# A graph network with gated updates: another order of the products with S, of the normalising and of the last step's VectorE work

## The chip, the cores and the metric

The kernel runs on one core of a Trainium2 chip. The metric is the device time of one execution in microseconds (us). Engines are named as in the profile: PE is TensorE, ACT is ScalarE, DVE is VectorE, POOL is GpSimd, SP is the queue that issues most DMAs.

## The reference

Eight graphs of 1024 nodes with 128 channels pass four layers of message passing with a gated unit (GRU); then the input is added and each node is normalised over its channels.

```python
h = x
for i in range(L):                                   # L = 4
    hw = jnp.einsum('bnc,cd->bnd', h, weight[i])
    m = jnp.einsum('bjn,bjd->bnd', adj, hw)          # 1024 x 1024 adjacency, 0 or 1
    gx, gh = m @ w_ih[i].T + b_ih[i], h @ w_hh[i].T + b_hh[i]
    r = sigmoid(xr + hr); z = sigmoid(xz + hz); n = tanh(xn + r * hn)
    h = (1 - z) * n + z * h
y = x + h * mask[:, :, None]
out = (y - mean(y)) / sqrt(var(y) + 1e-5)            # over the 128 channels
```

## The kernel before

**Tiling and stages.** Graphs go in four pairs (`p` = 0 to 3, here also "pair 1" to "pair 4"). A pair takes eight steps `g` = 0 to 7: layer `g // 2` of graph `g % 2`, so that one graph's matmuls run while the other's state is made and turned. The layer's weight is folded into the input weights (`wx`) at the start. Every value that TensorE reads is split in two, a rounded high part and the remainder (`nat_hi`, `nat_lo` for the state in natural layout; `hT_hi`, `hT_lo` for the transposed state; `S_hi`, `S_lo` for the aggregated state), because one pass of TensorE rounds its operands.

**A step on TensorE.** `aggregate` makes S, the neighbours' sum, for both halves of 512 nodes: 32 matmuls with 128x512 results (line 465). Then `gates` runs for each half `h`: nine matmuls with the state, into p_r, p_z and p_hn, and nine with S, into p_r, p_xn and p_z (`product`, lines 476 to 478, three each). The four result banks are shared by both halves, so the second half's first matmul into a bank waits until the first half's reader has emptied it: `r_act`, `z_act`, `t_mul`, `t_add`.

**What the other engines do with a half.** ScalarE: sigmoid of p_r, sigmoid of p_z, and, after VectorE, tanh (`gate`, line 657). VectorE: (p_hn + bias) * r (line 1094), that plus p_xn (line 1100). POOL: h - n (line 1212), times z (line 1216). VectorE: `new_state`, n + that (line 923), `turn`, a transposition of 32x32 blocks (line 865); SP sends it to DRAM (`bounce`) and back (`low`, also called `back`) in natural layout, ScalarE and VectorE split it (`take_back`). ScalarE and VectorE also make S_hi (line 602) and S_lo (`s_low`, line 808), hT_hi and hT_lo, and ScalarE copies or checks the adjacency of the next graphs (`take_adj`, `check_adj`).

**The end of a graph.** In steps 7 (graph 0) and 0 of the next pair (graph 1) VectorE adds the input (`residual`, line 881), takes statistics (line 892) and moments (line 901), POOL raises the variance to the power -1/2 (line 1195). `normalise` (line 912) runs at the end of VectorE's steps 1 (graph 0 of the former pair) and 2 (graph 1), eight instructions each; SP stores in steps 2 and 3 and loads the next x into `y` in step 4.

**The last step** of the last pair has its own order by hand (`last_step` on PE, ACT and DVE): there S is made for half 0, its gates, then for half 1. Graph 0's normalising is ScalarE's work: `shift` (line 1013) is made by VectorE from POOL's power, and ScalarE waits for it (`shift_made`) with two blocks ahead of the sigmoids of half 1 (lines 671 and 693).

**What sets the order.** All engines work through their instructions in the order of the program and wait on semaphores; nothing reorders them. SP's queue is one such order too.

Of the kernel before, what the change touches and what calls it, by code (L numbers as in the profile page):

```python
# [34 lines left out]
def gnn_kernel(nc, x, adj, nodemask, weight, w_ih, w_hh, b_ih, b_hh, out):  # L35
    B, N, C = x.shape
    L = weight.shape[0]
    NB = N // P
# [10 lines left out]
    with ctx:  # L49
# [219 lines left out]
        def _(sp):  # L269
# [30 lines left out]

            def send_back(p, g, first):

                for h in range(2):
                    n = STEPS * p + g
                    sp.wait_ge(h_turned, HS * p + 2 * g + h + 1)
                    if not (first and g == 0):
                        sp.wait_ge(bounce_back[h], 16 * n)
                    sp.dma_start(bounce[h], turned[:, h]).then_inc(bounce_out[h], 16)

                    if first and g == 0:  # L310
                        sp.wait_ge(low_first, 1)
                    elif g == 0:
                        sp.wait_ge(y_added, 4 * (p - 1) + 2 + h + 1)
                    elif g == STEPS - 1:
                        sp.wait_ge(y_added, 4 * p + h + 1)
                    else:
                        sp.wait_ge(nat_split, HS_IN * p + 2 * (g - 1) + h + 1)
                    sp.wait_ge(bounce_out[h], 16 * (STEPS * p + g + 1))
                    sp.dma_start(back[:, h].rearrange("p q j c -> p q (j c)"),
                                 bounce[h].rearrange("(q r) (m f) -> (r m) q f", q=Q, m=Q)).then_inc(bounce_back[h], 16)  # L320

            def body(p, first, last):
                for g in range(STEPS):
# [4 lines left out]
                    if g in (2, 3):  # L328
                        if not last:
                            next_adj(p, 0, first, range((g - 2) * HB, (g - 1) * HB))  # L330
                        if not first:
                            store(p - 1, g - 2)
                    elif g == 4:
# [3 lines left out]
                        for s in range(2):  # L337
                            if not first:

                                sp.wait_ge(out_stored[s], 16 * p)  # L340
                            sp.dma_start(y[:, s], x_v[2 * p + s]).then_inc(y_loaded[s], 16)
                    elif last:
# [33 lines left out]
        def _(pe):  # L376
# [103 lines left out]
            def gates(p, g, h, first, between=None):  # L480
# [22 lines left out]
                product(p_r, (wx_hi, wx_lo), l, 0, fed, False, True).then_inc(r_done, 1)  # L503
                if prior:
                    pe.wait_ge(t_add, HS * p + k)
                product(p_xn, (wx_hi, wx_lo), l, 2, fed, True, True).then_inc(xn_done, 1)
                product(p_z, (wx_hi, wx_lo), l, 1, fed, False, True).then_inc(z_done, 1)
# [297 lines left out]
        def _(dve):  # L805
# [103 lines left out]
            def normalise(p, s):  # L909
                dve.wait_ge(rstd_made, 2 * p + s + 1)  # L910
                for j in range(NB):
                    last = nc.vector.tensor_scalar(y[:, s, j], y[:, s, j], mv[:, s, j, 0:1], rstd[:, s, j:j + 1],  # L912
                                                   ALU.subtract, ALU.mult)
                last.then_inc(y_normed, 1)
# [80 lines left out]
            def last_step(p):  # L995
                g = STEPS - 1
                k = 2 * g
                whole = slice(0, H)
                new_state(p, g - 1, 1)
                turn(p, g - 1, 1)  # L1000
                s_low(p, g, 0)
# [3 lines left out]
                residual(p, 0, 1)  # L1005
                for h in range(2):
                    wait_stats(p, 0, h)
                    moments(0, h)
                variance_eps(p, 0)
                s_low(p, g, 1)  # L1010
                new_state(p, g, 0)
                dve.wait_ge(rstd_made, B - 1)
# [34 lines left out]
            def body(p, first, last):  # L1047
# [4 lines left out]
                def fill():  # L1052
                    if checks:
                        check_adj(*checks.pop(0))
                        if not checks:
                            mask_first()

                for g in range(STEPS):
# [25 lines left out]
                    for h in range(2):  # L1084
# [16 lines left out]
                        if h == 0:  # L1101
# [4 lines left out]
                            elif g:  # L1106
                                take_back(p, g - 1, 1)
                            if last and g == STEPS - 2:
# [16 lines left out]
                    if 1 <= g <= 2 and not first:  # L1125

                        normalise(p - 1, g - 1)
# [135 lines left out]
```

## Time and profile before

| | |
|---|---|
| time, median of 3 runs | 562.23 us (562.16 to 562.79) |
| the profiled execution | 565.01 us, its span 563.1 us |
| PE busy | 528.3 us, 94% |
| DVE busy | 416.0 us, 74% |
| ACT busy | 357.1 us, 63% |
| POOL busy | 213.3 us, 38% |
| mean granted clock of PE | 0.987 of full speed |

The span is the time from the first to the last instruction that the profiler recorded; the profiled execution's own time has the start and the end around it. A matmul's busy time is longer than its share of the stream, since matmuls overlap: 390 ns each, while the next one starts 0.23 us after it. So the busy share of PE hides short stalls, and distances between starts show them.

### The profile page before, as it was taken

The page shows a single profiled execution, that of the slowest core. Times are in us where ns is not written, and L with a number is a line of the kernel's source. Part 1 is how long each engine was busy: PE and PEld are TensorE (multiplying, and loading weights), DVE is VectorE, ACT ScalarE, POOL GpSimd, SP SyncE. Part 2 cuts the span into 40 slices and gives each one's busy share as a digit, 9 for nine tenths or more (in the row PEclk, how much of TensorE's full clock was granted, in tenths as well). Part 3 has the DMA queues.
Part 4 walks back from the last instruction along what each step waited for, and adds up shares of the span by engine and source line. Part 5 has one row for each costly group of instructions (what it writes and reads, how often), then busy time and mean ns, then how long its engine had stood idle before and what let it go on. Part 6 is the DMA issues. An engine that isn't in the chain of part 4 may idle for free.

```text
span 563.1 us, 7447 instructions
## 1 busy us (share of the span) xinstructions
PE 528.3 (94%) x2288; PEld 419.1 (74%) x2288; DVE 416.0 (74%) x737; ACT 357.1 (63%) x568; POOL 213.3 (38%) x161
## 2 busy tenths in 40 slices
PE   5898999999999999999999999999999999999981
PEld 4566788778887777778787777777888777887660
DVE  3997766765888786676788777667688778767586
ACT  3856767647776667755877576755886764544332
POOL 0143333333365333322366431332365522433332
PEclk9999999999999999999999999999999999999986
DMA  7952445443722177544541176643471133341112
GB/s 228 393 185 75 154 182 177 142 131 131 275 81 76 56 244 243 150 130 150 192 182 56 56 240 196 197 148 113 134 258 38 57 112 112 101 120 61 59 36 78
DMA packets 79808, 80.93 MB, mean 144 GB/s; under 512 B 3656, under 2 KB 63648, under 8 KB 79776
## 3 DMA queue, kind: packets, MB, share of 16 engines
q1 hardware_dynamic: 79504, 80.41, 43.1%
q8 instruction: 16, 0.26, 0.2%
q10 hardware_dynamic: 272, 0.13, 0.1%
q14 instruction: 16, 0.13, 0.1%
HBM read 60.08 MB, written 20.45 MB: 143 GB/s over the span
## 4 chain that ended last, share of the span: by engine, by line
PE 45%; DVE 24%; ACT 13%; issue 7%; DMA 5%; POOL 3%; SPq 2%; DVEq 1%; ACTq 0%; POOLq 0%
PE p_S L465 18%; ACT work L657 6%; ACT adj_hi L602 4%; PE p_z L476 4%; DVE y L912 3%; DVE work L1094 3%; PE p_r L476 3%; PE p_z L478 3%; PE p_z L477 3%; DVE work L1100 3%; PE p_r L478 3%; DMA low<-bounce 3%; PE p_r L477 3%; DVE hT L923 2%; DVE hT_lo L808 2%
## 5 line engine op out<-in xcount | busy, mean ns | idle before, releaser
L1212 POOL TENSOR_TENSOR work<-hT,work 128x512 f32<-128x512 f32 x63 | 82.7, 1313 | 295.3 <-ACT work L657 295.3
L465 PE MATMUL p_S<-adj_hi,nat_hi 128*128 128x512 f32 x480 | 187.3, 390 | 0.0
L465 PE MATMUL p_S<-adj_hi,nat_lo 128*128 128x512 f32 x480 | 186.8, 389 | 0.0
L465 PEld LDWEIGHTS p_S<-adj_hi,nat_lo 128*128 128x128 f32 x480 | 90.1, 188 | 18.6
L465 PEld LDWEIGHTS p_S<-adj_hi,nat_hi 128*128 128x128 f32 x480 | 90.1, 188 | 18.5
L1094 DVE SCALAR_TENSOR_TENSOR work<-p_hn,bias,work 128x512 f32<-128x512 f32 x62 | 46.6, 751 | 76.0 <-ACT work L657 75.7
L1216 POOL TENSOR_TENSOR work<-work 128x512 f32<-128x512 f32 x63 | 89.7, 1423 | 4.9
L602 ACT ACTIVATE S_hi<-p_S 128x512 fp32r<-128x512 f32 x64 | 37.9, 592 | 64.0 <-PE p_S L465 59.2
L865 DVE STREAM_TRANSPOSE work<-hT 128x512 f32<-128x512 f32 x62 | 69.0, 1112 | 2.1
L923 DVE TENSOR_TENSOR hT<-work 128x512 f32<-128x512 f32 x63 | 43.2, 686 | 32.9 <-POOL work L1216 32.9
L657 ACT ACTIVATE work<-work,bias 128x512 f32<-128x512 f32 x63 | 45.4, 721 | 30.7 <-DVE work L1100 29.6
L657 ACT ACTIVATE work<-p_r,bsum 128x512 f32<-128x512 f32 x63 | 43.0, 683 | 34.1 <-PE p_r L478 34.0
L657 ACT ACTIVATE work<-p_z,bsum 128x512 f32<-128x512 f32 x64 | 44.0, 687 | 29.1 <-PE p_z L478 29.1
L602 ACT ACTIVATE adj_hi<-adj_in 128x1024 fp32r<-128x1024 f32 x60 | 60.6, 1049 | 0.5 <-DMA adj_in<-in_adj_dram 0.4
L629 ACT ACTIVATE low_words<-adj_in 128x1024 bf16<-128x1024 uint16 x56 | 58.4, 1043 | 0.0
L1100 DVE TENSOR_TENSOR work<-p_xn,work 128x512 f32<-128x512 f32 x62 | 42.5, 685 | 5.2
L808 DVE TENSOR_TENSOR S_lo<-p_S,S_hi 128x512 fp32r<-128x512 f32 x64 | 43.0, 672 | 1.3 <-ACT S_hi L602 1.3
L808 DVE TENSOR_TENSOR nat_lo<-low,nat_hi 128x512 fp32r<-128x512 f32 x48 | 34.5, 719 | 11.5 <-ACT nat_hi L602 11.5
L808 DVE TENSOR_TENSOR hT_lo<-hT,hT_hi 128x512 fp32r<-128x512 f32 x48 | 41.3, 860 | 0.0
L602 ACT ACTIVATE hT_hi<-hT 128x512 fp32r<-128x512 f32 x48 | 30.0, 624 | 12.3 <-DVE hT L923 11.9
L1204 POOL TENSOR_TENSOR hT<-hT_hi,hT_lo 128x512 f32<-128x512 f32 x16 | 24.8, 1570 | 33.7 <-DVE hT_lo L808 33.7
L602 ACT ACTIVATE nat_hi<-low 128x512 fp32r<-128x512 f32 x48 | 30.1, 628 | 10.6 <-DMA low<-bounce 10.4
(149 smaller groups left out, 919.8 us busy)
## 6 DMA issues: line engine op xcount, KB each, us to landing
adj_in<-in_adj_dram SPq DMA_DIRECT2D x64, 512.0 KB, 6.3
bounce<-work SPq DMA_DIRECT2D x62, 256.0 KB, 2.0
low<-bounce SPq DMA_DIRECT2D x62, 256.0 KB, 2.8
x_in<-in_x_dram SPq DMA_DIRECT2D x8, 512.0 KB, 4.6
y<-in_x_dram SPq DMA_DIRECT2D x8, 512.0 KB, 4.8
out_dram<-y SPq DMA_DIRECT2D x7, 512.0 KB, 7.9
y<-in_L_gnn_w_ih_dram SPq DMA_DIRECT2D x2, 192.0 KB, 3.4
y<-in_L_gnn_w_hh_dram SPq DMA_DIRECT2D x2, 192.0 KB, 3.8
```

The source lines that it names most:

```text
L465: last = nc.tensor.matmul(p_S[h][:, :], part[:, s, j], adj_hi[:, s, j, half(h)], start=(j == 0 and part is nat_hi), stop=(j == NB - 1 and ...
L476: nc.tensor.matmul(bank[:, :], w_h[:, l, cols], v_h, start=start, stop=False)
L602: return nc.scalar.activation(dst, src, ACT.Copy)
L629: nc.scalar.activation(low_words[:, :], adj_in[:, j].bitcast(U16)[:, ::2], ACT.Copy, accum_out=low_sums[:, bass.ds(NB * (2 * p + s) + j, 1 ...
L657: nc.scalar.activation(dst, bank, func, bias=b).then_inc(made, 1)
L808: return nc.vector.tensor_tensor(dst, src, hi.bitcast(F32), ALU.subtract)
L865: nc.vector.transpose(turned[:, h].rearrange("p (m j c) -> p m j c", m=Q, j=HB), hT[:, g % 2, half(h)].rearrange("p (j r m) -> p m j r", j ...
L923: nc.vector.tensor_tensor(hT[:, g % 2, half(h)], n_sb[:, h], t_sb[:, h], ALU.add).then_inc(h_new, 1)
L1094: nc.vector.scalar_tensor_tensor(t_sb[:, h], p_hn[:, :], bias[:, 1, G * l + 2:G * l + 3], r_sb[:, h], ALU.add, ALU.mult).then_inc(t_mul, 1)
L1100: nc.vector.tensor_tensor(t_sb[:, h], p_xn[:, :], t_sb[:, h], ALU.add).then_inc(t_add, 1)
L1212: nc.gpsimd.tensor_tensor(t_sb[:, h], hT[:, s, half(h)], n_sb[:, h], ALU.subtract).then_inc(d_sub, 1)
L1216: nc.gpsimd.tensor_tensor(t_sb[:, h], z_sb[:, h], t_sb[:, h], ALU.mult).then_inc(d_mul, 1)
```

## The change

Three edits. `gates` issues the products with S in the order r, z, xn (the wait for `t_add` goes with xn). `normalise` takes a range of blocks: graph 0 of the former pair is normalised in steps 1 and 2, graph 1 in steps 3 and 4, two blocks in the middle of each step and two at its end; SP stores graph 0 in step 3 and graph 1 in step 5, and loads y for graph 0 in step 4 and for graph 1 in step 6. In VectorE's last step `s_low` for half 0 stands first, and `s_low` for half 1 and the new state of half 0 stand ahead of the second residual with its statistics.

```diff
--- before.py
+++ after.py
@@ -298,6 +298,12 @@
                 sp.wait_ge(y_normed, 2 * p + s + 1)
                 sp.dma_start(out_v[2 * p + s], y[:, s]).then_inc(out_stored[s], 16)
 
+            def load_y(p, s, first):
+                if not first:
+
+                    sp.wait_ge(out_stored[s], 16 * p)
+                sp.dma_start(y[:, s], x_v[2 * p + s]).then_inc(y_loaded[s], 16)
+
             def send_back(p, g, first):
 
                 for h in range(2):
@@ -328,18 +334,19 @@
                     if g in (2, 3):
                         if not last:
                             next_adj(p, 0, first, range((g - 2) * HB, (g - 1) * HB))
-                        if not first:
-                            store(p - 1, g - 2)
+                        if g == 3 and not first:
+                            store(p - 1, 0)
                     elif g == 4:
                         if first:
 
                             sp.wait_ge(start_tr, L)
-                        for s in range(2):
-                            if not first:
-
-                                sp.wait_ge(out_stored[s], 16 * p)
-                            sp.dma_start(y[:, s], x_v[2 * p + s]).then_inc(y_loaded[s], 16)
-                    elif last:
+                        load_y(p, 0, first)
+                    elif g == 5:
+                        if not first:
+                            store(p - 1, 1)
+                    elif g == STEPS - 2:
+                        load_y(p, 1, first)
+                    if last:
                         pass
                     elif g == 5:
                         for s in range(2):
@@ -501,10 +508,10 @@
                     between()
                 pe.wait_ge(s_split, HS * p + k + 1)
                 product(p_r, (wx_hi, wx_lo), l, 0, fed, False, True).then_inc(r_done, 1)
+                product(p_z, (wx_hi, wx_lo), l, 1, fed, False, True).then_inc(z_done, 1)
                 if prior:
                     pe.wait_ge(t_add, HS * p + k)
                 product(p_xn, (wx_hi, wx_lo), l, 2, fed, True, True).then_inc(xn_done, 1)
-                product(p_z, (wx_hi, wx_lo), l, 1, fed, False, True).then_inc(z_done, 1)
 
             def low_total():
 
@@ -906,12 +913,13 @@
                 dve.wait_ge(y_aggr, 2 * p + s + 1)
                 nc.vector.tensor_scalar(vare[:, s], mv[:, s, :, 1], EPS, None, ALU.add).then_inc(var_eps, 1)
 
-            def normalise(p, s):
+            def normalise(p, s, blocks):
                 dve.wait_ge(rstd_made, 2 * p + s + 1)
-                for j in range(NB):
+                for j in blocks:
                     last = nc.vector.tensor_scalar(y[:, s, j], y[:, s, j], mv[:, s, j, 0:1], rstd[:, s, j:j + 1],
                                                    ALU.subtract, ALU.mult)
-                last.then_inc(y_normed, 1)
+                if blocks.stop == NB:
+                    last.then_inc(y_normed, 1)
 
             def s_low(p, g, h):
                 dve.wait_ge(s_hi_made, HS * p + 2 * g + h + 1)
@@ -996,19 +1004,20 @@
                 g = STEPS - 1
                 k = 2 * g
                 whole = slice(0, H)
+                s_low(p, g, 0)
                 new_state(p, g - 1, 1)
                 turn(p, g - 1, 1)
-                s_low(p, g, 0)
                 residual(p, 0, 0)
                 gated(p, k, 0, whole)
                 candidate(p, k, 0, whole)
-                residual(p, 0, 1)
-                for h in range(2):
-                    wait_stats(p, 0, h)
-                    moments(0, h)
-                variance_eps(p, 0)
+                wait_stats(p, 0, 0)
+                moments(0, 0)
                 s_low(p, g, 1)
                 new_state(p, g, 0)
+                residual(p, 0, 1)
+                wait_stats(p, 0, 1)
+                moments(0, 1)
+                variance_eps(p, 0)
                 dve.wait_ge(rstd_made, B - 1)
                 nc.vector.scalar_tensor_tensor(shift[:, :], mv[:, 0, :, 0], -1.0, rstd[:, 0], ALU.mult,
                                                ALU.mult).then_inc(shift_made, 1)
@@ -1054,6 +1063,11 @@
                         check_adj(*checks.pop(0))
                         if not checks:
                             mask_first()
+
+                def part_of(g, n):
+
+                    i = 2 * ((g - 1) % 2) + n
+                    return range(i * (NB // 4), (i + 1) * (NB // 4))
 
                 for g in range(STEPS):
                     l, s = divmod(g, 2)
@@ -1105,6 +1119,8 @@
                                 wait_stats(*ended, 1)
                             elif g:
                                 take_back(p, g - 1, 1)
+                            if 1 <= g <= 4 and not first:
+                                normalise(p - 1, (g - 1) // 2, part_of(g, 0))
                             if last and g == STEPS - 2:
                                 dve.wait_ge(low_sum, 1)
                                 nc.vector.tensor_scalar(flag[0:1, :], p_S[0][0:1, 0:1], 0.0, None,
@@ -1122,9 +1138,8 @@
                         h_low(p, g, 0)
                     if first and g == 0:
                         take_adj1(5)
-                    if 1 <= g <= 2 and not first:
-
-                        normalise(p - 1, g - 1)
+                    if 1 <= g <= 4 and not first:
+                        normalise(p - 1, (g - 1) // 2, part_of(g, 1))
                     fill()
                     if last and g == STEPS // 2:
                         mask_low()
```

## Rows read from the trace of the kernel before

**Rows 1.** Waits of TensorE, whole span: total us, times, longest us

```profile
PE p_r L476 <- DVE S_lo L808: 3.1, 4, 1.4
...
PE p_r L476 <- ACT work L657: 2.2, 6, 0.4
...
PE p_r L476 <- DVE hT_lo L808: 2.0, 3, 0.7
```

**Rows 2.** Timeline, TensorE: start, length, line, out<-in, [idle before <-releaser]

```profile
68.39 0.50 PE L476 MATMUL p_z<-hT_hi,wh_hi 128*128 128x512 f32 x1
...
507.52 0.39 PE L478 MATMUL p_r<-hT_hi,wh_lo 128*128 128x512 f32 x1
508.01 0.50 PE L476 MATMUL p_z<-hT_hi,wh_hi 128*128 128x512 f32 x1
508.35 0.39 PE L477 MATMUL p_z<-hT_lo,wh_hi 128*128 128x512 f32 x1
```

**Rows 3.** Timeline of ScalarE and VectorE, pair 4, step 5, first half

```profile
505.97 0.69 ACT L657 ACTIVATE work<-p_r,bsum 128x512 f32<-128x512 f32 x1 [1.66 <-PE p_r L478]
...
507.27 0.69 ACT L657 ACTIVATE work<-p_z,bsum 128x512 f32<-128x512 f32 x1 [0.61 <-PE p_z L478]
...
506.76 0.75 DVE L1094 SCALAR_TENSOR_TENSOR work<-p_hn,bias,work 128x512 f32<-128x512 f32 x1 [1.65 <-ACT work L657]
...
507.62 0.69 DVE L1100 TENSOR_TENSOR work<-p_xn,work 128x512 f32<-128x512 f32 x1
```

**Rows 4.** Timeline of POOL, VectorE and TensorE, pair 3, steps 2 and 3

```profile
336.43 1.62 POOL L1216 TENSOR_TENSOR work<-work 128x512 f32<-128x512 f32 x1
...
336.82 3.10 DVE L912 TENSOR_SCALAR y<-y,mv,rstd 128x128 f32<-128x128 f32 x8
...
339.86 0.67 DVE L923 TENSOR_TENSOR hT<-work 128x512 f32<-128x512 f32 x1
...
342.31 0.50 PE L476 MATMUL p_r<-S_hi,wx_hi 128*128 128x512 f32 x1 [0.65 <-DVE S_lo L808]
```

**Rows 5.** Timeline of VectorE, pair 4, start of step 6

```profile
516.66 0.69 DVE L923 TENSOR_TENSOR hT<-work 128x512 f32<-128x512 f32 x1 [1.18 <-POOL work L1216]
```

**Rows 6.** Page, part 6 (us to landing last); timeline of SP and ScalarE

```profile
adj_in<-in_adj_dram SPq DMA_DIRECT2D x64, 512.0 KB, 6.3
...
390.56 5.12 SPq L295 DMA_DIRECT2D adj_in<-in_adj_dram  x2
...
410.24 1.05 ACT L602 ACTIVATE adj_hi<-adj_in 128x1024 fp32r<-128x1024 f32 x1
```

**Rows 7.** Timeline of ScalarE and TensorE, from pair 3's step 6 to pair 4's step 1

```profile
395.51 0.69 ACT L657 ACTIVATE work<-p_r,bsum 128x512 f32<-128x512 f32 x1 [0.40 <-PE p_r L478]
...
411.32 0.69 ACT L657 ACTIVATE work<-p_r,bsum 128x512 f32<-128x512 f32 x1
...
438.17 0.50 PE L476 MATMUL p_r<-hT_hi,wh_hi 128*128 128x512 f32 x1 [0.70 <-DVE hT_lo L808]
```

**Rows 8.** Timeline of VectorE, POOL and ScalarE, last step

```profile
535.25 1.14 DVE L881 SCALAR_TENSOR_TENSOR y<-low,mask,y 128x128 f32<-128x128 f32 x4 [0.72 <-DMA low<-bounce]
...
539.08 3.30 DVE L881 SCALAR_TENSOR_TENSOR y<-low,mask,y 128x128 f32<-128x128 f32 x4 [0.34 <-DMA low<-bounce]
...
544.54 0.68 DVE L923 TENSOR_TENSOR hT<-work 128x512 f32<-128x512 f32 x1
...
545.80 0.17 DVE L1013 SCALAR_TENSOR_TENSOR shift<-mv,rstd 128x8 f32<-128x8 f32 x1 [0.57 <-POOL rstd L1195]
...
540.95 1.29 POOL L1216 TENSOR_TENSOR work<-work 128x512 f32<-128x512 f32 x1
...
544.12 1.65 POOL L1195 TENSOR_TENSOR rstd<-vare,mhalf 128x8 f32<-128x8 f32 x1 [1.88 <-DVE vare L907]
...
547.50 0.84 ACT L693 ACTIVATE work<-p_r,bsum 128x256 f32<-128x256 f32 x2 [0.63 <-PE p_r L478]
...
549.63 0.69 ACT L657 ACTIVATE work<-p_z,bsum 128x512 f32<-128x512 f32 x1 [1.29 <-PE p_z L478]
```

## The prediction

> **What bounds the kernel now.** I began with busy times: TensorE is busy 94% of the span, so a change pays only where TensorE waits. The table of its waits comes next [rows 1]: 3.1 us for S_lo, 2.2 us for the sigmoid of r, 2.0 us for hT_lo. That table leaves out short stalls, so I went through TensorE's timeline and took the distance from start to start. A 128x512 matmul follows the one before it by 0.22 to 0.23 us; wherever the distance is longer, TensorE stood still, whatever the busy column says. The commonest stall is not in the table at all. In the second half-step the first p_z product with the state starts 0.49 us after its predecessor and the next one 0.34 us later [rows 2]: 0.26 + 0.11, or 0.36 us lost, with the rounding. Its cause is z_act: the products with S are issued r, xn, z, so z's sum is ready last; its sigmoid starts at 507.27 and ends at 507.96, and p_z can be overwritten only then [rows 3]. From 56 us on, 22 first p_z products have such a gap (21 of 0.36 us, one of 0.19); the first and the last of them stand in the rows.
>
> The third view is the timeline of steps 2 and 3 of a pair. There a whole former graph is normalised at the end of the VectorE step before, eight instructions in 3.10 us. POOL's product, for which the new state waits, ended at 338.05; the state was made at 339.86 because VectorE was still normalising, 1.8 us late. S_lo is late behind it, TensorE waits for it, and then for r's sigmoid, which ScalarE reaches late behind its copies [rows 1, 4]. The fourth view is the chain of waits around the hT_lo wait (below), the fifth the last step.
>
> **The change part by part.** The sum is made in microseconds off the profiled execution, 565.01 us for a span of 563.1; the median of the runs is 562.23, and I take the same amount off it.
>
> *1. Order r, z, xn.* No instruction is added. Take R for the start of the last r product of the first half. From the trace, R = 505.48 (0.49 before the sigmoid of r at 505.97 [rows 3]), the r sigmoid runs R+0.49 to R+1.18. z's sum is now ready 3 x 0.23 = 0.68 us earlier, so z's sigmoid starts as the r sigmoid leaves ScalarE, about R+1.16 instead of R+1.79, and ends at R+1.85. The waiting p_z product would be due at R+2.27 (ten matmuls on). With 0.05 to 0.13 us for the release it is no longer late; 0.3 us remain. So 0.36 us go wherever nothing else is late. What gets later: xn's sum, by 0.68 us, to R+1.85. Its reader, the second VectorE operation, starts at 507.62 = R+2.14 because it comes behind the first [rows 3]; 0.3 us of cover, cost nothing. Were this cover gone, tanh, POOL's products and the state would be later by the excess.
>
> *2. Normalising in four parts.* 48 normalising instructions stay 48 (three former pairs). Steps 1 and 2 lose six of eight at their end; steps 1 to 4 have two in the middle and two at the end. At 3.10/8 = 0.39 us each a part is 0.78 us. In the middle it stands before the second half's first operation, where VectorE idles 1.65 us for the r sigmoid in the like place [rows 3]; at the end before the new state, where VectorE idles 1.18 us for POOL when nothing is normalised [rows 5]. Both fit, so both parts cost nothing, and the 1.8 us lateness in steps 2 and 3 goes. By gap, what goes with it: before S_lo and its follower 0.22, 0.92 (pair 4), 0.11, 0.91 (pair 3), 0.11, 0.71 (pair 2) = 3.0 us; before p_r with its follower (the r sigmoid) 0.57, 0.59, 0.60, 0.17, 0.60, 0.61, 0.25, and 0.10 at the p_z after the last = 3.5 us. The table has the longer ones of them: four waits before S_lo, of which the longest, 1.4 us, is the last step's, and six for r's sigmoid, of which one is pair 1's and stays [rows 1]; one of the S_lo waits has its row [rows 4]. Total 6.5 us. Next late in those steps would be z_act, which part 1 has moved.
>
> *3. The queue.* SP sends the first former graph off one step later, the second two steps later, and loads y's second half in step 6, ahead of two adjacency blocks. A 512 KB block lands 6.3 us after its issue, and a load ahead of it delays it by at most that much again. The first block issued from 390.56 on is copied by ScalarE at 410.24 [rows 6]: 19.7 - 6.3 = 13.4 us to spare, so nothing. Stores wait for y_normed at steps 3 and 5, one step after its last part, so SP doesn't block the state's way through DRAM.
>
> *4. Where the z gain is swallowed.* The hT_lo wait in step 1 stays. The chain of waits leads from it without any TensorE work, over VectorE, POOL and ScalarE, through all of steps 7 and 0 (adjacency copies, residual, statistics), back to the r sigmoid at 395.51, which last waited for TensorE [rows 7]. That is 42.6 us whose length the change doesn't touch: TensorE arrives earlier at the wait and waits longer. The z gaps of steps 7 and 0 lie in it in each of three pairs: six of the 22 gaps bring nothing. Left are 15 x 0.36 + 0.19 = 5.6 us.
>
> *5. The last step.* S_lo for the first half goes ahead of new_state; TensorE then doesn't wait its longest S_lo wait, 1.4 us. But the chain behind doesn't start there: the first residual still waits for its DMA until 535.25, gated and candidate stand behind it, so tanh and POOL's product end at 542.24 as before [rows 8]. S_lo for the second half is made while POOL works, and the new state follows POOL at once, at 542.27 instead of 544.54: 2.3 us earlier. Behind it now come the second residual (1.14 us if POOL is idle, as in the first), four statistics, four moments and the variance (1.4 us together, an estimate: from the end of the residual at 542.38 to the power at 544.12 VectorE did these with four moments more, and POOL's start): POOL's power starts at 545.5 instead of 544.12, shift is ready at 547.2 instead of 545.80. And ScalarE waits for shift, with two normalising instructions, ahead of the r sigmoids of the second half: these start at 548.2 instead of 547.50. z's sigmoid, which began at 549.63 for its own late sum, now directly follows them at 549.0. VectorE gets through gated and candidate 0.7 us later, at 550.3, just when z's sigmoid used to end (549.63 + 0.69) and the operation on it to begin. So 2.3 us earlier at TensorE, nothing at the end: -0.1 to +0.1, taken as 0.
>
> The second residual has a price with two ends: 1.14 us (alone) and 3.30 us (as it ran from 539.08, with POOL's two products from 539.58 to 542.24) [rows 8]. I take 1.14, since after 542.24 POOL has nothing until the power; 3.30 would delay shift and the end by 2.2 us.
>
> By the Trainium skill, "SBUF — State Buffer", section "Who interferes with whom", a VectorE instruction with two SBUF inputs contends with a GpSimd instruction that reads SBUF, and the later one is blocked. The trace agrees in that the slow residual is the one beside POOL. The same rule speaks against the parts of the normalising, each of which now falls beside POOL's products: blocking POOL for two of them would be the third rival.
>
> **Sum.** 5.6 + 6.5 + 0 = 12.1 us. 565.01 - 12.1 = 552.9 for a profiled execution, and 562.23 - 12.1 = 550.1 us at the median.
>
> **The rivals.**
> *A, the r/z order doesn't get swallowed.* If the chain of part 4 also shortens (r's sigmoid in steps 7 and 0 earlier), six gaps of 0.36 us come back: 2.2 us more, 547.9. Against it: the r sigmoid at 411.32, in step 7, has no wait for TensorE before it [rows 7]. Chance 0.07.
> *B, the last step takes more.* The residual at 3.30 us, or a longer wait of ScalarE for shift: +2.2 us, 552.3. Chance 0.10.
> *C, the parts get in the way or the edit does less than it says.* If ScalarE is late in steps 2 to 4 for its own adjacency checks and not for the state, the r waits (3.5 us) stay, and 550.1 + 3.5 = 553.6; POOL held up under each of the twelve end parts for 0.78 us would make the new state that much late and bring back at most as much of the S_lo and r waits. For it: several r sigmoids in steps 3 and 4 directly follow a check. Against: the checks themselves stand behind copies that waited for the state. Chance 0.11.
> *D, slower.* SP's queue: the y load and the stores push the next pair's adjacency back, and the 42.6 us chain, whose start is adjacency copies, gets longer. It decides once the delay exceeds the 13.4 us to spare [rows 6]; two transfers of 6.3 us are 12.6 us, just short of that. If each of three pairs lost a third one, 550.1 + 18.9 = 569.0 us. Chance 0.02.
> *The forecast:* 0.70.
>
> **How the numbers follow.** The range reaches from A's time, 547.9, past B's 552.3 to 552.8; what it leaves out is the full C and D, 0.13, and the edges of the unknown prices. A measurement of this kernel can tell a difference of about 0.2%, 1.1 us, from none. All but D are faster by more; I keep 0.01 for a cancelling of gains.
>
> **What the next profile would show.** Right: first p_z products in steps 1 to 6 at 0.23 us behind their predecessor; z's sigmoid right behind r's; no S_lo wait in steps 2 and 3; the hT_lo wait of step 1 still there three times, and longer, about 1.4 us against 0.7; in the last step no wait before p_r, about 2 us before the transposes, shift later than the new state by some 4 us, r's sigmoid pair waiting for shift. Wrong: a new gap before p_hn (the first VectorE operation late) in step 1 to 6, a wait of VectorE's second operation for xn, or r sigmoids in steps 2 to 4 still late behind checks. The sum falls if the z gap returns at another product.

## The result, and the profile after

The changed kernel takes 558.11 us at the median (six executions, 555.42 to 559.86) against 562.53 (562.16 to 563.55) for the kernel before: a ratio of 0.9906, 95% interval 0.9878 to 0.9933. Of the 12.1 us predicted, that is 4.4 by the medians and 5.3 (3.8 to 6.9) by the ratio. Executed again in the experiments, beside other executions of before, the same kernel gave 0.9861 (0.983 to 0.9892): 7.2 us by the medians, 7.8 (6.1 to 9.6) by the ratio. The two intervals overlap. The direction held and the size did not. The profiled execution took 555.42 us, its span is 553.6. The changed lines of the page (part 1 and groups of part 5; the columns are busy us, mean ns of one, and idle before it):

```profile
span 553.6 us, 7447 instructions
PE 520.9 (94%) x2288; PEld 420.8 (76%) x2288; DVE 436.6 (79%) x737; ACT 354.3 (64%) x568; POOL 213.7 (39%) x161
...
L919 DVE TENSOR_SCALAR y<-y,mv,rstd 128x128 f32<-128x128 f32 x48 | 45.5, 988 | 0.0
...
L664 ACT ACTIVATE work<-p_z,bsum 128x512 f32<-128x512 f32 x64 | 43.9, 686 | 0.0
```

Two readings lie in it. z's sigmoid (L664 from p_z) has no idle time before it any more: it follows r's directly. And a normalising instruction (L919) takes 988 ns in the mean, where the prediction took 390. The table of TensorE's waits (total us, times, longest) answers [rows 1]:

```profile
PE p_tr L527 <- DVE hT L1044: 5.6, 1, 5.6
...
PE p_r L483 <- DVE hT_lo L815: 2.8, 3, 1.0
PE p_tr L438 <- DVE hT L931: 2.1, 1, 2.1
...
PE p_hn L483 <- DVE work L1108: 1.2, 3, 0.5
PE p_r L483 <- ACT work L664: 1.1, 3, 0.4
...
PE p_r L483 <- DVE S_lo L815: 0.7, 2, 0.4
```

The waits for S_lo and for r's sigmoid are shorter (3.1 and 2.2 us before), but not gone; the hT_lo wait is there three times, as before, and longer; p_hn is new; and two waits of the last step's transposes head the list.

As the table leaves out short stalls, one number is used below for all kernels, **the stalls**: over TensorE's timeline from 56 to 515 us, each distance from start to start less 0.227 us for each 128x512 matmul in it, summed where it exceeds 0.04 us. The distances to and from the 128x128 transposes are left out, and so are the start phase and the last step. It is 17.6 us in the trace of before, of which 7.9 stand at p_z; 9.7 in the trace of the change, of which none stands at p_z. (A "follower" is the next matmul, whose start is still 0.1 us late.)

**Where the gain went.** The timeline of the change in pair 2, step 2, for VectorE, POOL and ScalarE. The two instructions in the middle of the step are called its middle part, the two at its end its end part.

```profile
195.47 0.69 DVE L815 TENSOR_TENSOR nat_lo<-low,nat_hi 128x512 fp32r<-128x512 f32 x1 [0.25 <-ACT nat_hi L609]
196.08 2.79 DVE L919 TENSOR_SCALAR y<-y,mv,rstd 128x128 f32<-128x128 f32 x2
198.79 0.74 DVE L1108 SCALAR_TENSOR_TENSOR work<-p_hn,bias,work 128x512 f32<-128x512 f32 x1
...
202.93 1.57 DVE L919 TENSOR_SCALAR y<-y,mv,rstd 128x128 f32<-128x128 f32 x2
204.42 0.68 DVE L931 TENSOR_TENSOR hT<-work 128x512 f32<-128x512 f32 x1
...
196.13 1.29 POOL L1227 TENSOR_TENSOR work<-hT,work 128x512 f32<-128x512 f32 x1 [8.40 <-ACT work L664]
197.49 1.29 POOL L1231 TENSOR_TENSOR work<-work 128x512 f32<-128x512 f32 x1
...
202.54 1.62 POOL L1231 TENSOR_TENSOR work<-work 128x512 f32<-128x512 f32 x1
...
196.99 0.67 ACT L664 ACTIVATE work<-p_r,bsum 128x512 f32<-128x512 f32 x1
...
200.36 0.72 ACT L664 ACTIVATE work<-work,bias 128x512 f32<-128x512 f32 x1 [2.09 <-DVE work L1114]
```

The middle part, two instructions, starts at 196.08 and ends at 198.87, right behind POOL's second product (198.78): 2.79 us for what was costed at 0.78. The r sigmoid that VectorE's next operation (L1108) waits for was done at 197.66, so that operation starts about 1.0 us late, and tanh behind it on ScalarE. The end part takes 1.57 us, ends behind POOL's product (204.16), and the new state starts 0.26 us after that product instead of at once. TensorE pays for it in the next steps (its stalls there, starts with the idle time):

```profile
223.63 0.50 PE L483 MATMUL p_r<-S_hi,wx_hi 128*128 128x512 f32 x1 [0.40 <-DVE S_lo L815]
...
226.33 0.47 PE L483 MATMUL p_r<-hT_hi,wh_hi 128*128 128x512 f32 x1 [0.37 <-ACT work L664]
```

The prediction's 390 ns was a mean that hid this. The summary of the same 48 instructions (shortest, median, longest in ns; first and last start) reads, in the trace of before and then in that of the change:

```profile
L912 DVE TENSOR_SCALAR y<-y,mv,rstd x48: 329/334/1314, 189.2 to 470.6; 128x128 f32<-128x128 f32 x48
```

```profile
L919 DVE TENSOR_SCALAR y<-y,mv,rstd x48: 331/1310/1450, 180.3 to 493.4; 128x128 f32<-128x128 f32 x48
```

In the kernel before, one instruction in a group of eight takes 1.31 us and the others go by 0.26 us apart: 3.10 us [rows 4]. In the changed one 30 of the 48 take the long time: each of the 12 end parts has one such instruction, seven of the 12 middle parts have two, four have one and one has none.

### The profile page after: what moved, and what is told of

The parts are those of the page before. It is cut to its first block, busy times and chain, and to the rows that moved or that the text cites. A ratio compares the mean times of both kernels' runs of the same rounds, so it can differ in the third digit from the quotient of the medians.

```text
span 553.6 us, 7447 instructions
## 1 busy us (share of the span) xinstructions
PE 520.9 (94%) x2288; PEld 420.8 (76%) x2288; DVE 436.6 (79%) x737; ACT 354.3 (64%) x568; POOL 213.7 (39%) x161
## 4 chain that ended last, share of the span: by engine, by line
PE 31%; DVE 30%; ACT 12%; issue 11%; DMA 9%; POOL 5%; SPq 2%; DVEq 1%; POOLq 0%; ACTq 0%
PE p_S L472 13%; DMA low<-bounce 6%; ACT work L664 4%; DVE work L1108 4%; ACT adj_hi L609 4%; DVE y L919 4%; DVE work L1114 4%; DVE hT_lo L815 3%; DVE hT L931 3%; DVE S_lo L815 3%; POOL work L1231 2%; POOL work L1227 2%; PE p_r L483 2%; PE p_r L485 2%; PE p_r L484 2%
## 5 line engine op out<-in xcount | busy, mean ns | idle before, releaser
L664 ACT ACTIVATE work<-work,bias 128x512 f32<-128x512 f32 x63 | 45.5, 722 | 63.8 <-DVE work L1114 60.1
L1108 DVE SCALAR_TENSOR_TENSOR work<-p_hn,bias,work 128x512 f32<-128x512 f32 x62 | 46.5, 749 | 48.9 <-ACT work L664 48.5
L664 ACT ACTIVATE work<-p_r,bsum 128x512 f32<-128x512 f32 x63 | 42.9, 680 | 21.5 <-PE p_r L485 21.5
L919 DVE TENSOR_SCALAR y<-y,mv,rstd 128x128 f32<-128x128 f32 x48 | 45.5, 988 | 0.0
L664 ACT ACTIVATE work<-p_z,bsum 128x512 f32<-128x512 f32 x64 | 43.9, 686 | 0.0
```

The costliest lines, as they stand in the source:

```text
L664: nc.scalar.activation(dst, bank, func, bias=b).then_inc(made, 1)
L1108: nc.vector.scalar_tensor_tensor(t_sb[:, h], p_hn[:, :], bias[:, 1, G * l + 2:G * l + 3], r_sb[:, h], ALU.add, ALU.mult).then_inc(t_mul, 1)
```

## The experiments

All were compared with executions of before on the same chip in the same stretch of time. Its median was 563.93 us beside `again`, `order`, `spread` and `idle_place`, 563.67 beside `last`, `before_look` and the two kernels with the old last step put back, and 563.48 beside `middle_moved` and `end_moved`. Two theories stood against the prediction's own account and each other. **Theory one:** the parts of the normalising, beside POOL's products, take 1.6 to 2.8 us, which makes tanh and the new state late; the rival is that the r/z order or SP's queue brought less than costed. **Theory two:** the last step's new order costs 2 to 2.5 us against the form in which before usually runs; the rival is that it is neutral, as predicted.

**The change again.** No edit.

> The changed kernel once more, unaltered. Theory one (a normalising instruction beside one of POOL's two products waits for that product's end, and which of the two comes first differs from run to run): times between 555 and 560 us again, with the median near 558, several us wider than the kernel before; in the trace some pairs of normalising instructions take 2.8 us, some 1.6 us, some 0.6 us, and not the same ones as in the first trace. Rival (the spread of the first six times came from that chip or hour): all within 1 us of 555.4.

Measured: 556.72 us (555.59 to 557.85), ratio 0.9861 (0.983 to 0.9892); the trace has 10.4 us of stalls against 9.7, two at S_lo in pair 4 among them (0.46 and 0.97 us, followers left out) that the first trace has nowhere. The mean of a normalising instruction is 1014 ns here. The traces differ in pair 4 in just this: its middle parts in steps 2 and 3 were held once in the first trace of the change and twice in this one. First trace, then this one:

```profile
454.26 1.57 DVE L919 TENSOR_SCALAR y<-y,mv,rstd 128x128 f32<-128x128 f32 x2
...
469.99 1.57 DVE L919 TENSOR_SCALAR y<-y,mv,rstd 128x128 f32<-128x128 f32 x2
```

```profile
454.97 2.81 DVE L919 TENSOR_SCALAR y<-y,mv,rstd 128x128 f32<-128x128 f32 x2
...
471.43 2.79 DVE L919 TENSOR_SCALAR y<-y,mv,rstd 128x128 f32<-128x128 f32 x2
```

**Only the order r, z, xn.** The kernel before with

```diff
                 product(p_r, (wx_hi, wx_lo), l, 0, fed, False, True).then_inc(r_done, 1)
+                product(p_z, (wx_hi, wx_lo), l, 1, fed, False, True).then_inc(z_done, 1)
                 if prior:
...
                 product(p_xn, (wx_hi, wx_lo), l, 2, fed, True, True).then_inc(xn_done, 1)
-                product(p_z, (wx_hi, wx_lo), l, 1, fed, False, True).then_inc(z_done, 1)
```

> The kernel before with nothing but the order r, z, xn of the products with S. If the sum of the prediction holds for this part: 5.6 us less, 556.9 us, all gaps before p_z in steps 1 to 6 gone, those of steps 7 and 0 swallowed by a longer wait for hT_lo, and times as narrow as those of the kernel before (about 1 us). If the swallowing is wrong: 2.2 us less again, 554.7. If the spread of times comes with the order (the gates' products closer to a bank's release): 3 us wide or more.

Measured: 555.86 us (554.46 to 558.42), ratio 0.9857 (0.9824 to 0.9891), 8.1 us. The stalls are 11.3 us: 6.3 less than before, none of them at p_z, while those for S_lo and r stay:

```profile
208.95 0.51 PE L476 MATMUL p_r<-S_hi,wx_hi 128*128 128x512 f32 x1 [0.49 <-DVE S_lo L808]
212.07 0.47 PE L476 MATMUL p_r<-hT_hi,wh_hi 128*128 128x512 f32 x1 [0.76 <-ACT work L657]
```

This one edit reaches the whole change's time. Either the other two bring nothing together, or one takes what the other gives.

**Only the normalising in parts, with SP's edits.** The changed kernel with the old order of the products and the old last step.

> The kernel before with nothing but the normalising over four steps, with its stores and loads. Theory one: the parts beside POOL cost 1.6 to 2.8 us each instead of 0.78, so of the 6.5 us little is left: 559 to 563 us, and the spread of times of several us is here. The prediction's own count, were the parts 0.78 us: 6.5 us less the p_z gaps that come back in steps 2 to 4 (six of 0.36): 558.2, narrow. Rival (the stores and loads in other steps delay the state's way through DRAM): the waits of ScalarE for the state from DRAM grow beyond 3 us at a time.

Measured: 561.69 us (560.18 to 565.19), ratio 0.9966 (0.9941 to 0.9991): 2 us, where the prediction's count gives 6.5, or 4.3 with the p_z gaps that come back in the old order. The stalls are 16.3 us. From its page:

```profile
L919 DVE TENSOR_SCALAR y<-y,mv,rstd 128x128 f32<-128x128 f32 x48 | 51.2, 1105 | 0.0
```

**The normalising where VectorE idles and POOL does too.** The changed kernel, with all four instructions of a step together in the first half-step, ahead of the operation that waits for r's sigmoid:

```diff
                                 take_back(p, g - 1, 0)
+                            if 1 <= g <= 4 and not first:
+                                normalise(p - 1, (g - 1) // 2, half_of(g))
                         dve.wait_ge(hn_done, HS * p + k + 1)
...
                                 take_back(p, g - 1, 1)
-                            if 1 <= g <= 4 and not first:
-                                normalise(p - 1, (g - 1) // 2, part_of(g, 0))
...
-                    if 1 <= g <= 4 and not first:
-                        normalise(p - 1, (g - 1) // 2, part_of(g, 1))
                     fill()
```

Here `half_of(g)` gives blocks 0 to 3 or 4 to 7.

> The changed kernel, but each step's four normalising instructions stand together ahead of the first half's first VectorE operation, where POOL has nothing to do; SP's stores and loads as in the change. Theory one: the four take 1.05 us together (0.26 each), no S_lo wait in steps 2 to 4, the full gain: 549.5 to 550.5 us, and times within 1 us. Rival, ScalarE's adjacency checks make r's sigmoid late: the r waits of steps 3 and 4 stay and the time is 553 or more. Rival, stores and loads make the spread: as wide as the changed kernel.

Measured: 552.19 us (550.47 to 553.01), ratio 0.9788 (0.9759 to 0.9818), 4.5 us below the change as it stands (`again`) on the same chip. The same stretch of its timeline, and its summary of the 48:

```profile
192.28 1.10 DVE L919 TENSOR_SCALAR y<-y,mv,rstd 128x128 f32<-128x128 f32 x4
193.53 0.75 DVE L1109 SCALAR_TENSOR_TENSOR work<-p_hn,bias,work 128x512 f32<-128x512 f32 x1
...
195.49 0.69 DVE L815 TENSOR_TENSOR nat_lo<-low,nat_hi 128x512 fp32r<-128x512 f32 x1 [0.41 <-ACT nat_hi L609]
197.78 0.75 DVE L1109 SCALAR_TENSOR_TENSOR work<-p_hn,bias,work 128x512 f32<-128x512 f32 x1 [1.60 <-ACT work L664]
```

```profile
L919 DVE TENSOR_SCALAR y<-y,mv,rstd x48: 331/339/352, 177.7 to 476.9; 128x128 f32<-128x128 f32 x48
```

Four instructions take 1.10 us where two took 2.79, and the operation in the second half-step starts at 197.78, a microsecond earlier. The stalls fall to 5.4 us. Theory one holds; since SP's edits and the order of the products are the same in both, it is not they that kept the gain back.

**Which of the two parts costs.** Two kernels, each the changed one with one of its parts moved to that idle place: the middle one (`middle_moved`) or the end one (`end_moved`). The first edit:

```diff
                                 take_back(p, g - 1, 0)
+                            if 1 <= g <= 4 and not first:
+                                normalise(p - 1, (g - 1) // 2, part_of(g, 0))
...
                                 take_back(p, g - 1, 1)
-                            if 1 <= g <= 4 and not first:
-                                normalise(p - 1, (g - 1) // 2, part_of(g, 0))
```

> The changed kernel with only the middle pair of normalising instructions moved ahead of the first half's first VectorE operation; the pair at the step's end stays. Theory: the middle pair (2.8 us beside POOL's two products, 1.0 us of it in front of the second half's first operation) is what costs, and the end pair (1.57 us) makes the new state only 0.3 us late: nearly the time of the run idle_place, 552 to 553.5 us, a ratio of 0.979 to 0.982 to the kernel before. If both pairs matter alike: half way, 554.5.

> The changed kernel with only the end pair moved ahead of the first half's first operation; the middle pair stays. Theory (the middle pair costs): little changes against the changed kernel, 555.5 to 557 us, a ratio of 0.984 to 0.987, with tanh of the second half still waiting 2.1 us for VectorE in steps 2 to 4. If the end pair is what costs: 552 to 553.

Measured: 552.45 us (550.86 to 553.06), ratio 0.9801 (0.9777 to 0.9826), stalls 5.6; and 551.87 us (550.79 to 555.06), ratio 0.98 (0.9771 to 0.9828), stalls 6.1. I had expected the middle part, the longer one, to cost by itself. It does not: with the end part moved it can still be held twice (2.83 us below), yet the state's wait for POOL is back, that is, VectorE is early again.

```profile
354.34 2.83 DVE L919 TENSOR_SCALAR y<-y,mv,rstd 128x128 f32<-128x128 f32 x2
357.10 0.74 DVE L1110 SCALAR_TENSOR_TENSOR work<-p_hn,bias,work 128x512 f32<-128x512 f32 x1
...
362.49 0.69 DVE L931 TENSOR_TENSOR hT<-work 128x512 f32<-128x512 f32 x1 [1.18 <-POOL work L1231]
```

Either lateness alone, about 1.0 us in the middle or 0.26 at the end, fits into the slack of a step; both together do not, and TensorE's S_lo and r stalls show it from step 3 on. One reservation: moving the end part also changed the race of the middle one, which was held twice in only five of 12 cases here, against seven to nine in the three traces of the change with both parts in place. But where it was held twice in two steps running (pair 2, steps 3 and 4, 2.80 and 2.81 us), no S_lo or r stall above 0.13 us followed. That the lateness adds up from step to step is my reading of where the stalls stand, not shown by a run of its own.

**Only the last step.** The kernel before with the new order in it:

```diff
+                s_low(p, g, 0)
                 new_state(p, g - 1, 1)
                 turn(p, g - 1, 1)
-                s_low(p, g, 0)
...
-                residual(p, 0, 1)
-                for h in range(2):
-                    wait_stats(p, 0, h)
-                    moments(0, h)
-                variance_eps(p, 0)
+                wait_stats(p, 0, 0)
+                moments(0, 0)
                 s_low(p, g, 1)
                 new_state(p, g, 0)
+                residual(p, 0, 1)
+                wait_stats(p, 0, 1)
+                moments(0, 1)
+                variance_eps(p, 0)
```

> The kernel before with nothing but the new order of VectorE's last step. The prediction: no change. Theory two: the profile that the prediction rests on caught a slow form of the old last step (second residual 3.30 us, 36.8 us from the r sigmoid of step 6's second half to the end); in most executions the residual is blocked by one POOL product instead of two (2.2 us) and the stretch takes 33.9 us as in the run spread, while the new order always takes 36.3. Then this kernel is 2 to 2.5 us slower than the kernel before.

Measured: 566.0 us (564.41 to 566.74, twelve executions), ratio 1.0033 (1.0011 to 1.0054). That is 2.3 us slower by the medians and 1.9 (0.6 to 3.0) by the ratio, not much more than the 1.1 us that can be told from none.

**The kernel before, once more** (`before_look`). No edit; it is for a second trace.

> The kernel before, unaltered, for a second trace. Theory two: time near 562.5 rather than 565; the second residual of the last step takes about 2.2 us, TensorE waits 1.3 us ahead of the transposes instead of 2.7 and keeps its full clock there, 33.9 us from the r sigmoid of step 6's second half to the end. If the old last step always takes the 36.8 us of the first trace, theory two falls.

Measured: 561.45 us, span 559.6. Its last step is not the one of [rows 8]:

```profile
538.32 2.17 DVE L881 SCALAR_TENSOR_TENSOR y<-low,mask,y 128x128 f32<-128x128 f32 x4 [0.23 <-DMA low<-bounce]
...
542.66 0.68 DVE L923 TENSOR_TENSOR hT<-work 128x512 f32<-128x512 f32 x1
543.91 0.17 DVE L1013 SCALAR_TENSOR_TENSOR shift<-mv,rstd 128x8 f32<-128x8 f32 x1 [0.57 <-POOL rstd L1195]
...
543.39 0.66 PE L431 MATMUL p_tr<-ident,hT 128*128 128x128 f32 x4 [1.32 <-DVE hT L923]
```

The second residual takes 2.17 us instead of 3.30 (it starts 0.60 us ahead of POOL's first product instead of 0.50), state and shift come earlier, and TensorE waits 1.32 us for the state instead of 2.68. From the r sigmoid of step 6's second half to the end of the span it is 33.9 us here, 36.8 in the first trace of before. This stretch is called the tail. The new order takes 36.4 (`last`) and 36.3 (the change); four other traces with the old order give 33.4 (order), 33.9 (spread), 33.5 (the changed kernel with the old last step) and 34.9 (the idle place with it; this one has the slow residual, 3.26 us). So the new order ends about as late as the slow form of the old at its worst, and 2.4 to 3.0 us behind the quick one. What it waits for is shift: counted from the same r sigmoid, shift starts at 21.1 us in the change and at 18.2 in `before_look`, and the last r sigmoids start at 22.0 and 19.2.

The 36.8 us hold two things that happened together. The trace with the slow residual and 34.9 us has the same late state (TensorE waits 2.70 us there, 2.68 in the first trace of before), but its TensorE runs on at full clock (the rows are in the last section). The two waits, the first trace of before ahead:

```profile
545.28 0.84 PE L431 MATMUL p_tr<-ident,hT 128*128 128x128 f32 x4 [2.68 <-DVE hT L923]
```

```profile
533.22 0.66 PE L438 MATMUL p_tr<-ident,hT 128*128 128x128 f32 x4 [2.70 <-DVE hT L931]
```

In the first trace of before the clock falls behind the wait, and the sigmoids that wait for the products are later: r's last ones start 21.2 us after the reference sigmoid instead of 20.5, and z's starts 2.1 us behind r's instead of 1.3 in `before_look`. Against the quick traces with the same order of products (33.4 and 33.5) the slow residual costs 1.4 to 1.5 us. The rest of the 2.9 us between 36.8 and 33.9, some 1.4 to 1.5 us, is by this estimate the low clock's.

**The old last step in the changed kernel, and in the one with the idle place** (`change_old_last`, `idle_place_old_last`): the edit above, undone.

> The changed kernel with its last step put back. Theory two: 2 to 2.9 us less than the changed kernel, 554 to 555 us. If the last step is neutral: 556.5 to 558.

> The order r, z, xn and the four normalising instructions together ahead of the first half's first VectorE operation, with the old last step. Theory two: about 2.5 us less than the same kernel with the new last step (552.2 on the chip before), so 549.5 to 550, the fastest so far; 33.4 us from the r sigmoid of step 6's second half to the end. If the last step is neutral, as predicted: no difference from 552.

Measured: 556.34 us (555.44 to 556.81), ratio 0.9869 (0.9841 to 0.9898), and 550.14 us (547.49 to 553.19), ratio 0.9759 (0.9724 to 0.9794). The second is the fastest kernel of the study, 13.5 us below before; the interval of its ratio overlaps that of idle_place (0.9788), so a gain over it isn't shown. The first misses the gain I had expected of it: the ratio is that of the change as it stands (0.9861). Its trace has the short tail (33.5 us against 36.3) but 11.5 us of stalls against 10.4 and 9.7, and a normalising mean of 1039 ns: the 1.1 to 1.8 us more of stalls take back part of the 2.8 it won in the last step. Whether its other executions did the same, their times alone don't tell.

## Why the prediction was wrong

*Part 1, order r, z, xn: right, and a little more.* Every p_z gap went, z's sigmoid follows r's. 5.6 us predicted, 6.3 us fewer stalls in the trace of that edit alone, 8.1 us (6.1 to 9.9) in its times. The 1.8 us between the two are within the interval; if there is more than noise in them, it lies outside the stretch I summed, and no run shows where.

*Part 2, normalising: wrong in the price of a part, and this is the main error.* The step that failed is "At 3.10/8 = 0.39 us each a part is 0.78 us", and with it "Both fit, so both parts cost nothing". The eight instructions of [rows 4] are one of 1.31 us, held until POOL's product ended, and seven unhindered. A part beside POOL is mostly held once (1.57 or 1.70 us) or twice (2.79 us). Of the 6.5 us predicted the parts brought 0.9 to 1.6 on top of part 1 in two traces (stalls 11.3 to 10.4 and 9.7), nothing in a third (11.5, the old last step put back) and 1.3 without part 1 (17.6 to 16.3, with 0.9 more at p_z). And the same instructions where POOL is idle brought 5.9 (11.3 to 5.4). The sum of both parts, predicted at 12.1, would have been right with the parts in that place: 17.6 to 5.4 is 12.2 us of stalls. (The median fell by 11.7 us, but that has the dearer last step in it.)

The idle time was there, then, and long enough for instructions at their own speed (1.60 us in idle_place at 197.78); what wasn't asked is what else runs in it. The 1.65 us of [rows 3] were read in the first half-step, where POOL has nothing to do (in that trace from 500.81 to 509.17), and carried over to "the like place" of the second, where POOL's products of the first half fall. The idle place of the experiments is the one that the row showed. The Trainium skill has the rule, in "SBUF — State Buffer", section "Who interferes with whom": among the kinds that can enter a two-port mode it names `tensor_scalar`, and whoever comes first holds the shared ports for its whole instruction while the other is fully blocked. The trace agrees in the blocking: the two instructions of 196.08 end 0.09 us after POOL's second product. In the order it agrees only roughly: VectorE's part starts 0.05 us ahead of POOL's product, at 196.13, and is held all the same. The prediction cited the section for two SBUF inputs, which a normalising instruction doesn't have, and looked at POOL as the one that would be held, for 0.78 us at most (a branch of rival C). POOL's products take 1.29 us each in the blocked stretch, as where no part stands beside them (196.15 us of idle_place: 1.29); the 1.62 us at 202.54 are no lengthening, since 25 products of idle_place take as long with no part beside them. VectorE paid.

*Part 3, the queue: right.* idle_place has all of SP's edits and the full gain.

*Part 4, the swallowed z gaps: right.* The hT_lo wait stayed, three times, and grew from 2.0 to 2.8 us in total (0.92, 0.92 and 0.97); the 1.4 predicted for each came in two pieces, the other being a new stall of p_hn in step 0 (0.25, 0.58 and 0.63 us), which the prediction didn't see. In the trace after, p_hn's stalls (1.8 us, followers included) and the growth at hT_lo (0.8) make 2.6 us for the 2.2 that six gaps were worth. Rival A fell.

*Part 5, the last step: about right against its own basis, which was the wrong one.* Shift, state, residual and the end came as computed: counted from the same r sigmoid, shift was to come at 547.2 and came at 547.3, and the second residual took 1.13 us (predicted 1.14). In the trace of the change:

```profile
533.31 0.69 DVE L931 TENSOR_TENSOR hT<-work 128x512 f32<-128x512 f32 x1 [1.53 <-POOL work L1231]
533.92 1.13 DVE L888 SCALAR_TENSOR_TENSOR y<-low,mask,y 128x128 f32<-128x128 f32 x4
...
538.34 0.17 DVE L1022 SCALAR_TENSOR_TENSOR shift<-mv,rstd 128x8 f32<-128x8 f32 x1 [1.76 <-POOL rstd L1210]
...
538.54 0.88 ACT L678 ACTIVATE y<-y,shift,rstd 128x128 f32<-128x128 f32 x2 [7.48 <-DVE shift L1022]
539.32 0.81 ACT L700 ACTIVATE work<-p_r,bsum 128x256 f32<-128x256 f32 x2
```

But the profiled execution was 2.8 us above the median, 565.01 against 562.23, and the step that failed is "I take the same amount off it". Of the 3.6 us between the two traces of before, 2.9 lie in the last step, which was in its slow form in the first, with the residual of 3.30 us, the long wait before the transposes and the fallen clock. An edit that only removes the slow form gains nothing where it isn't there, and this one puts shift behind the second residual, with ScalarE's r sigmoids behind shift: +1.9 to +2.3 us in the times of `last`, +2.5 in its trace against `before_look`. Rival B had the price (2.2 us) and, with "a longer wait of ScalarE for shift", the mechanism. How often before takes its slow form isn't known, since there are only two traces of it. Its times do go with the clock: of the 45 executions in the experiments, the 11 with a mean granted clock of 0.992 or more took 561.5 to 563.2 us, and the six with 0.984 took 566.1 to 567.7; where in the kernel the clock fell in them isn't recorded.

Together: stalls 7.2 to 7.9 us fewer, last step 2.3 us more, so 4.9 to 5.6 us; the two measurements, 5.3 and 7.8 us by their ratios (4.4 and 7.2 by the medians), lie about it. The weak term is the last step's: its cost stands clear of noise only in the kernel that has nothing else changed. The changed kernel with the old last step put back (0.9869) was no faster than the change as it stands (0.9861), and that is open. Why the change's own executions spread over 4.4 us is not settled. The three traces of its normalising order them as their means do (988, 1014, 1039 ns for 9.7, 10.4, 11.5 us of stalls), and pair 4 shows it within one kernel, so the races with POOL are probably a part of it; three traces don't settle how large a part.

## What to carry to other kernels

A group's mean in a profile is no price for its instructions at another place: look at shortest, median and longest, and if one of eight takes four times as long, find what ran beside it. Before work is put into an idle stretch of VectorE, check what POOL does in that stretch; one half-step earlier the same instructions were free. And where the profiled execution differs from the median, find the stretch in which it does before costing an edit to that stretch.

## What the runs showed of the hardware

VectorE's tensor_scalar on 128x128 fp32 blocks takes 0.33 to 0.35 us beside an idle POOL (1.10 us for four in a row) and 1.31 to 1.46 when it is held by one of POOL's fp32 products; two took 2.79 us. A four-instruction residual with two SBUF inputs took 1.14 us alone and 2.17 or 3.30 beside one or two of them.

Which of the two is held goes by a tenth of a microsecond. Over all traces of this study, a normalising instruction was held whenever POOL's product started 0.02 to 0.09 us after it (90 cases). Where the product started 0.10 us or more after it (20 cases, while it ran), it kept its 0.34 us, and the product took at most 1.39 us instead of 1.29.

The granted clock in the last step: the columns are the stretch, busy us of PE, PEld, DVE, ACT and POOL with their instructions, the clock, and the DMA's share and GB/s. The first pair of rows is the new last step, in the two traces of the change, behind waits of TensorE of 2.14 and 2.09 us. The second pair is the old last step with the slow residual, in the first trace of before and in `idle_place_old_last`, behind waits of 2.68 and 2.70 us.

```profile
534.00:539.00 5.00, 4.01 (x13) 2.73 (x13) 3.14 (x18) 0.46 (x2) 1.65 (x1) 0.66 0.00 0
```

```profile
536.40:541.40 5.00, 2.72 (x13) 2.00 (x13) 3.14 (x17) 0.52 (x2) 1.65 (x1) 1.00 0.00 0
```

```profile
545.00:550.00 5.00, 4.31 (x13) 3.20 (x13) 3.06 (x10) 2.09 (x5) 0.76 (x1) 0.66 0.01 2
```

```profile
533.00:538.00 5.00, 2.74 (x13) 2.01 (x13) 4.18 (x16) 3.66 (x9) 2.29 (x3) 1.00 0.01 3
```

0.66 is a mean over a stretch partly at 1.2 GHz and partly at 2.4 GHz; 1.00 is 2.4 GHz throughout. So nearly the same wait is followed by a low clock in one execution and by the full clock in another; the wait's length alone doesn't decide it. What it costs depends on what waits for TensorE. In the new last step the r sigmoids wait for shift in any case, and the tail took 36.3 us at the low clock and 36.4 at the full one. In the old one r's and z's last sigmoids wait for the products, and the tail took 36.8 and 34.9, of which about 0.5 is the order of the products (33.9 against 33.4 in the quick traces). So the 1.9 to 2.3 us that the new order costs are not the clock's.
